# A graph network and a mixture-of-experts layer on one core: turned one-hots kept in DRAM after the first layer instead of being made again in each of the three

## The reference

```
z = (x @ W).reshape(N, heads, dim)
el, er = sum(z * al), sum(z * ar)
e = leaky_relu(el[src] + er[dst]);  ex = exp(e - m[dst])
alpha = ex / segment_sum(ex, dst)[dst]
out = segment_sum(alpha * z[src], dst) + z + bias
```

## Time and profile before

| | us |
|---|---|
| median of 3 runs | 2811.04 (2809.19 to 2813.04) |
| span of the profiled execution | 3059.8 |
| gathers of the first layer, first to last (POOL L672) | 246 to 884 |
| gathers of the second layer | 1103 to 1740 |
| gathers of the third layer | 1954 to 2590 |

### The profile page before, as it was taken

One profiled execution on the slowest core, in us unless ns is written; L12 is line 12 of the kernel. 1 busy time (PEld: TensorE's weight loads), 2 busy tenths in 40 slices (PEclk: granted clock), 3 DMA queues, 4 the chain that ended last, 5 costly groups with the idle time before them and its releaser, 6 DMA issues.

```text
span 3059.8 us, 57119 instructions
## 1 busy us (share of the span) xinstructions
PE 2691.3 (88%) x14056; PEld 1838.6 (60%) x14060; DVE 2096.8 (69%) x3895; ACT 1244.9 (41%) x2607; POOL 1506.0 (49%) x1528
## 2 busy tenths in 40 slices
PE   3997999998989979898989999788898889759998
PEld 2884555555558855555555578555555555547776
DVE  6776888888887768888878877545555555673332
ACT  1224555555544435555555544223222223622211
POOL 1005666666631156666666412466666665114443
PEclk9998999999999979999999999899999999979999
DMA  6447888888867878888888767788888887967776
GB/s 210 169 148 251 289 286 291 291 290 290 289 219 205 210 228 292 289 287 290 291 287 288 250 191 216 218 281 285 279 282 281 282 282 258 397 217 145 145 146 118
DMA packets 199261, 762.09 MB, mean 249 GB/s; under 512 B 41889, under 2 KB 58033, under 8 KB 198542
## 3 DMA queue, kind: packets, MB, share of 16 engines
q0 software_dynamic: 127632, 604.14, 64.8%
q1 hardware_dynamic: 53790, 108.21, 11.6%
q10 hardware_dynamic: 17760, 48.79, 4.0%
HBM read 640.01 MB, written 133.45 MB: 253 GB/s over the span
## 4 chain that ended last, share of the span: by engine, by line
PE 50%; DVE 21%; issue 13%; ACT 4%; DMA 4%; another core or an unknown queue 3%; SPq 2%; POOL 1%; DVEq 1%; ACTq 1%; POOLq 0%
PE PS L1047 30%; DVE arena L1492 5%; PE PS L1176 5%; PE PS L978 4%; PE PS L1165 4%; PE PS L980 2%; DVE parts L1509 2%; PE PS L1022 2%; DMA arena<-table,src_k 2%; SPq L493 1%; DVE ST_b L1445 1%; DVE arena L1357 1%; DVE arena L1367 1%; DVE arena L1335 1%
## 5 line engine op out<-in xcount | busy, mean ns | idle before, releaser
L672 POOL DMA_INDIRECT arena<-table,src_k x945 | 959.9, 1016 | 500.8 <-issue 213.1
L1047 PE MATMUL PS<-arena,S 128*128 128x384 f32 (+1 forms) x1848 | 706.8, 514 | 57.8 <-issue 46.3
L1492 DVE TENSOR_TENSOR arena<-arena,PS 128x768 f32<-128x768 f32 x630 | 575.2, 946 | 0.9 <-ACT arena L822 0.9
L1047 PEld LDWEIGHTS PS<-arena,S 128*128 128x128 f32 x1848 | 335.5, 194 | 282.7 <-issue 156.8
L1047 PE MATMUL PS<-parts,S 128*128 128x384 f32 (+2 forms) x1332 | 340.4, 375 | 57.2 <-issue 51.0
L672 POOL DMA_INDIRECT W<-table,src_k x300 | 295.9, 986 | 160.5 <-PE PS L1047 71.2
L1047 PE MATMUL PS<-arena,S_weighted 128*128 128x384 f32 (+1 forms) x840 | 319.9, 516 | 33.4 <-issue 25.3
L1022 PEld LDWEIGHTS PS<-erp,ST_b 128*128 128x128 bf16 x3735 | 193.9, 97 | 249.9 <-issue 184.2
L618 POOL DMA_DIRECT2D table<-arena x75 | 41.6, 555 | 557.7 <-DVEq L1379 382.3
L1047 PEld LDWEIGHTS PS<-parts,S 128*128 128x128 f32 x1332 | 223.7, 192 | 106.0 <-issue 97.5
L830 ACT ACTIVATE apart<-iota_row,dst_k 128x128 f32<-128x128 f32 x830 | 261.7, 389 | 60.8 <-issue 44.1
(11 more groups left out here) (293 smaller groups left out, 4354.1 us busy)
## 6 DMA issues: line engine op xcount, KB each, us to landing
arena<-mixed SPq DMA_DIRECT2D x63, 384.0 KB, 3.6
table<-arena POOLq DMA_DIRECT2D x50, 396.0 KB, 3.3
local_b<-local SPq DMA_DIRECT2D x123, 160.0 KB
mixed<-sums ACTq DMA_DIRECT2D x50, 384.0 KB
arena<-table SPq DMA_DIRECT2D x50, 384.0 KB, 4.6
arena<-table,src_k POOLq DMA_INDIRECT x945
table<-arena POOLq DMA_DIRECT2D x25, 384.5 KB, 4.6
out<-last_bias POOLq DMA_DIRECT2D x25, 384.0 KB, 6.4
```

The costliest lines, as they stand in the source:

```text
L672: nc.gpsimd.indirect_dma_start(edge_row(l, k % U)[:, 0:table_width(l)], None, table[l][:, :], bass.IndirectOffsetOnAxis(src_k[:, k:k + 1]. ...
L1047: o = nc.tensor.matmul(flat[:, bass.ds(odd * 1024 + 512 * c, n)], onehot, row[:, c * HALF:c * HALF + n], start=False, stop=True, skip_grou ...
L1492: nc.vector.tensor_tensor(z, z, a, ALU.mult).then_inc(s_msg, 1)
```

## The change

In the first layer VectorE makes the turned one-hots as before, and SP stores each pair of groups (128 partitions by 1280 bf16, 2560 bytes a partition) to a new DRAM tensor `turned_kept` of 13.6 MB. In the second and third layer VectorE makes none: SP loads the pairs back into `ST_b` in place of the bytes in `local_b` (1280 bytes a partition), and TensorE waits for that load instead of for VectorE. The load of a pair waits until TensorE has used the buffer (`s_er`); in the first layer VectorE waits for the store of the pair before it overwrites the buffer. Two small integer tables become bytes, and the block number gets an AND with 255 before it is added to a wait's count.

```
+        turned_kept = nc.dram_tensor("turned_kept", (P, NG, G * P), BF16, kind="Internal").ap()
...
-        b_g = sb("b_g", [1, NG, 4], I32)
+        b_g = sb("b_g", [1, NG, 4], U8)
...
+                def keep_turned(g):
+                    groups, jj = min(2, NG - g), g % NBUF
+                    sp.wait_ge(s_ST, g + groups)
+                    sp.dma_start(turned_kept[:, g:g + groups, :], ST_b[:, jj:jj + groups, :]).then_inc(s_kept_ST[jj // 2], 16)
+
+                if l == 1:
+                    for j in range(NBUF // 2):
+                        sp.wait_ge(s_kept_ST[j], 16 * len(range(2 * j, NG, NBUF)))
                 for g in range(0, NG, 2):
                     groups = min(2, NG - g)
-                    used = NG * l + max(0, g + groups - NBUF)
+                    used = max(0, g + groups - NBUF)
+                    jj = g % NBUF
+                    if l:
+                        sp.wait_ge(s_er, NG * l + used)
+                        sp.dma_start(ST_b[:, jj:jj + groups, :], turned_kept[:, g:g + groups, :]).then_inc(s_lb[jj // 2], 16)
+                        continue
                     if used:
                         sp.wait_ge(s_ST, used)
...
+                    if g >= NBUF:
+                        keep_turned(g - NBUF)
...
-                    if j == 0:
-                        pe.wait_ge(s_ST, g + (NG * l + 1))
+                    if j == 0 and l == 0:
+                        pe.wait_ge(s_ST, g + 1)
+                    if j == 0 and l:
+                        pe.wait_ge(s_lb[jj // 2], 16 * lap + 16 * (uses(jj - jj % 2) * l + 1))
...
-                    pe.wait_ge(s_acc_free, b + (NB * l + 1))
+                    pe.wait_ge(s_acc_free, (b & (LOW - 1)) + (NB * l + 1))
...
-                    dve.wait_ge(s_lb[jj // 2], 16 * i + 16 * (uses(jj - jj % 2) * l + 1))
+                    dve.wait_ge(s_lb[jj // 2], 16 * i + 16)
+                    if not isinstance(i, int) or i:
+                        dve.wait_ge(s_kept_ST[jj // 2], 16 * i)
...
-                        if j == 1 and turn_next:
+                        if j == 1 and turn_next and l == 0:
                             turned(g + NBUF, i + 1, jj)
...
+                    dve.sem_inc(s_columns)
+                for jj in range(NBUF if l == 0 else 0):
                     turned(jj, 0, jj)
-                turned(NBUF - 1, 0, NBUF - 1)
```

More of the change, by code:

```diff
@@ L29 @@
 ER_LEAD = 3
+LOW = 256
 U = G * NBUF
@@ L168, in gnn_ffn @@
         b_k = sb("b_k", [1, V + 1], I32)
-        b_g = sb("b_g", [1, NG, 4], I32)
+        b_g = sb("b_g", [1, NG, 4], U8)
         b_of = sb("b_of", [1, NG + ER_LEAD, 8], I32)
         ends = sb("ends", [1, NB], I32)
-        turns = sb("turns", [1, NS], I32)
+        turns = sb("turns", [1, NS], U8)
         erm = sb("erm", [P, NB, 2 * HMAX])
@@ L235, in gnn_ffn @@
         s_dl = sem("s_dl"); s_local = sem("s_local"); s_lb = [sem(f"s_lb{j}") for j in range(NBUF // 2)]
+        s_kept_ST = [sem(f"s_kept_ST{j}") for j in range(NBUF // 2)]
+        s_columns = sem("s_columns")
         s_S = sem("s_S"); s_apart = sem("s_apart"); s_ST = sem("s_ST"); s_er = sem("s_er"); s_pre = sem("s_pre")
@@ L531, in _ @@
                     sp.wait_ge(s_local, 16 * 4)
+                def keep_turned(g):
[5 more added lines that the diff above has]
+                        sp.wait_ge(s_kept_ST[j], 16 * len(range(2 * j, NG, NBUF)))
                 for g in range(0, NG, 2):
                     groups = min(2, NG - g)
-                    used = NG * l + max(0, g + groups - NBUF)
+                    used = max(0, g + groups - NBUF)
[4 more added lines that the diff above has]
+                        continue
                     if used:
                         sp.wait_ge(s_ST, used)
-                    jj = g % NBUF
                     sp.dma_start(local_b[:, jj:jj + groups, :].rearrange("p g e -> p (g e)"),
@@ L540, in _ @@
                                  ).then_inc(s_lb[jj // 2], 16)
+                    if g >= NBUF:
+                        keep_turned(g - NBUF)
+                if l == 0:
+                    for g in range((NG - 1) // 2 * 2 - NBUF + 2, NG, 2):
+                        keep_turned(g)
             for q in range(2):
@@ L1015, in blocks_of, with er_of_edges @@
                         skip_runtime_bounds_check_because="b(k) is a sum of NB - 1 comparisons")[1]
-                def er_of_edges(g, jj, j, b):
-                    if j == 0:
-                        pe.wait_ge(s_ST, g + (NG * l + 1))
+                def er_of_edges(lap, g, jj, j, b):
+                    if j == 0 and l == 0:
+                        pe.wait_ge(s_ST, g + 1)
+                    if j == 0 and l:
+                        pe.wait_ge(s_lb[jj // 2], 16 * lap + 16 * (uses(jj - jj % 2) * l + 1))
                     for part in range(3):
@@ L1062, in body @@
                                 for n in ((0, 1), (2, 3, 4))[j // 2]:
-                                    er_of_edges(g + ER_LEAD, (jj + ER_LEAD) % NBUF, n, later[n])
+                                    er_of_edges(i + (jj + ER_LEAD) // NBUF, g + ER_LEAD, (jj + ER_LEAD) % NBUF, n, later[n])
                 pe.wait_ge(s_erm, l + 1)
+                if H == 1:
+                    pe.wait_ge(s_columns, 1)
                 for g in range(ER_LEAD):
@@ L1068, in edge_sweep @@
                     for j in range(G):
-                        er_of_edges(g, g, j, now[j])
+                        er_of_edges(0, g, g, j, now[j])
                 with pe.Fori(0, NI - 1) as i:
@@ L1543, in edge_sweep @@
                     dc.link(o)
-                for jj in range(NBUF - 1):
+                    dve.sem_inc(s_columns)
+                for jj in range(NBUF if l == 0 else 0):
                     turned(jj, 0, jj)
-                turned(NBUF - 1, 0, NBUF - 1)
                 if H > 1:
```

## The result

The changed kernel takes 2829.57 us (median of 4 runs, 2825.21 to 2835.47), the kernel before beside it 2810.11 us (4 runs). The ratio is 1.0078, with an interval of 1.0059 to 1.0096: slower by about 20 us, where 2851 (2790 to 2895) had been forecast.

What follows compares the result with a forecast made beforehand. Transfers in flight were taken to set the pace, with POOL and VectorE waiting for late gathers. VectorE 0, stores and loads 40, waits 0 and AND 0 us, added to 2811, gave 2851 us, range 2790 to 2895.

Steps and rivals of the forecast that it cites:

- The AND: One register instruction more on TensorE for each of 1245 visits, taken at 0 because TensorE works behind VectorE.
- The bound of 62 us: Upper limit for the AND on TensorE: at most 50 ns for each of 1245 visits.
- Stores and loads: First layer's stores and later layers' loads: 40 us, three quarters of 55 us of DMA time.
- The DMA bill: DMA engine time by packets: 34.5 us for first-layer stores, 20 us for both later layers' loads, 55 us together.
- My own sign: First layer's first-to-last gather: if it kept its 637 us, the idle DMA time was free and the forecast wrong.
- the idle 12% are not free time that can be booked: DMA engines in the edge sweeps: store packets between a gather's packets make it late, so most of the bill is paid.
- The rule that I had set against my step: HBM limit of about 358 GB/s a core: 290 GB/s leave 68 free, so all added traffic would cost 0.
- VectorE's relief: 83 `turned` fewer in each of layers 2 and 3, 103 us of busy time, taken at 0 on the path.
- The faster rival: VectorE partly on the path (25 us) and gathers no longer lengthened by `turned` (12 us): 2779 us; chance 24%.
- The waits for the loads: TensorE's `er_of_edges` in layers 2 and 3: loads wanted 19 us later land within 9.0 us, cost 0.
- the signs that I read: Edge sweeps: POOL stood still 1.30 us and VectorE waited for late gathers, read as five gathers in flight at most.
- the 249 us between span and median: Timed median 248.8 us below the profiled span; guessed to lie in the edge sweeps, 40 us carried over unchanged.

Runs made afterwards that it cites:

- e1: Changed kernel without stores or loads of turned one-hots; VectorE makes them in every layer, AND and byte tables stay; 2831.56 us, 1.0066 of the kernel before.
- f1: e1 with ScalarE's table b_g in four-byte words again and its two numbers masked on ScalarE; 3083.45 us, 1.0062 of the kernel before on that chip.
- e2: e1 plus the first layer's stores of turned one-hots, which nobody reads; 2829.86 us, 1.0061 of the kernel before.
- f3: Changed kernel, AND kept, with TensorE's wait for the free sum bank ahead of its wait for the message; 3082.07 us, 1.0047 of the kernel before.
- f2: Changed kernel with AND and words; nothing stored or loaded, layers two and three make no turned one-hots; 3075.0 us, 1.0029 of the kernel before.

## Why the prediction was right in sign, inside its range by luck, and wrong in its cause

The forecast was slower by 40 us, 20 to 62; it came to 19.5, the lower edge. All 40 were for stores and loads, which on this sort of chip cost nothing that can be told, and what did cost was put at 0. That the sum still lay in its range is luck.

**The AND, taken at 0.** This is the step that failed. I wrote that it costs nothing because "TensorE works several us behind VectorE, its semaphores have been given". The lag was read rightly, but an engine that lags and has its inputs is held by its own pace, and that pace is the sequencer's. "The trace has no row for one" was wrong too: L1042 has 1245 rows. By them an instruction takes 93 to 97 ns of the sequencer, nearly twice the 50 ns of my bound. The bound of 62 us held for the first AND (17.8 us on chip A in e1, 17.5 on B in f1), not for the second (125 us). By size the first accounts for the whole difference of the changed kernel. The sequencer's rows show that it is full on chip A with the AND (10 to 16 us of pauses), and the second AND costs what its rows take. That the first costs 18 us rests on exclusion: e1 leaves out the traffic, f1 the byte table `b_g` too, on the other sort of chip. The kernel before with nothing but the AND was not run, nor the changed kernel without it and with words, and neither `turned_kept`'s place in DRAM nor the other small things were parted from it.

**Stores and loads, taken at 40 us.** The DMA bill itself was near. SP's queue went to 10.6% in the first layer (forecast 9%), and its packets rose by 6048 in the whole run (59838 against 53790), where I had counted 5312. My own sign, "if the first layer keeps its 637 us, the idle DMA time was free", came true: between the starts of its first and last gathers 560.4 us in e1 and 561.2 with the stores in e2, on chip B 641.1 in f1 and 641.8 in f3. The step from bill to path failed, "the idle 12% are not free time that can be booked". The rate simply went up: from 329 to 352 GB/s on chip A, from 287 to 307 on B. The rule that I had set against my step, in the Trainium skill (DMA: Bandwidth & Descriptors, Specifications), about 358 GB/s for a core at the HBM, would have hidden the whole bill; the trace agrees on that outcome, not on the limit, which one stretch exceeds (367 GB/s in the earlier trace rows). The same page of the Trainium skill (Measured, in its part on bandwidth) says that about 358 is what each gets when both cores of a pair stream, and no run here shows two.

**VectorE's relief, taken at 0.** Right, or nearly. It is at most 8.5 us on chip B in f2 against f1. In the profiled executions of the other sort, gathers of the third layer take 542.1 us in the changed kernel and 549.5 in e1, 7 us less; the sequencer has 40 rows fewer there, about 4 us of it. The faster rival's price of 37 us is far off. Relief and transfers together cancel: the changed kernel is within 6 us of e1.

**The waits for the loads, taken at 0.** Right. Loads land in 6.1 us, stores in 6.8, and no row of the profile after shows the er matmuls waiting for a load.

**What bounds the kernel.** For chip B the signs that I read stand: stops of POOL, late gathers. It was not the chip on which the kernel was timed. There POOL issues nearly without a stop, TensorE is at 0.95 and VectorE at 0.93 in the first layer of both e1 and the changed kernel, and with the AND TensorE's sequencer has no pauses left. I saw the 249 us between span and median and carried the 40 us over all the same. The guess that they lie in the edge sweeps was right: the three take 1662 us in the profile after.

**What stays open.** How the 18 us of the AND divide over the layers on chip A, and how near to full its sequencer is without the AND, since there is no trace of the kernel before from such a chip. Whether another order of waits, or a block number bounded without an extra instruction and without bytes, brings the 18 us back there: the first was tried on chip B only, the second not at all. And what the two sorts of chips differ in; only the rate of transfers and the stops show it. No version was found that beats the kernel before.

## What to carry to other kernels

If the span of a profile differs from the timed median by several per cent, the two come from different conditions, and a share of 0.88 or a stop read in one doesn't hold in the other; say first which of the two the change is timed in. Price every instruction that a change adds to the busiest engine's queue, register instructions too, before the large transfers that it is about: the small mask cost 18 us, the 27 MB more of traffic nothing that could be told on the chip of the timing. Look at the sequencer's own rows (PEldq here) for it: a TensorE that is busy for 0.95 doesn't say whether the array or the sequencer is full, and the pauses between those rows do. And measure such a side effect by leaving it in and taking the main part out, as e1 does; that one run overturned the story.

## What the runs showed of the hardware that was not expected

- A second register instruction per visit on TensorE cost 100 ns each time (125 us over 1245), while the first cost 14 ns (17.8 us). The trace has them 96 to 97 ns apart from the next row of the sequencer. With one AND it paused for 10 to 16 us in about 1590 us of edge sweeps on chip A, with two for 4 us in 1712. For the first AND on chip A, slack in the sequencer as the reason is not shown; on chip B its pauses fell from 322 to 214 us.
- Loading five block numbers into TensorE's registers took 1222 ns (median of 498) from a table of bytes and 582 ns from words. The stretch with two such loads grew by 0.86 us (4.24 to 5.10).
- The same kernel took 2811 us on one sort of chip and 3064 on the other. On each chip its 11 or 15 executions lay within 0.5% of each other. All of the difference that the traces show lies in the edge sweeps, where transfers ran at 329 GB/s (e1) against 287 (f1).
- A gather packet took 230 ns without (e1) and 218 ns with the stores' packets beside it (e2).
